# New step orders in the local transformers, and attention weights turned inside the normalisation

## Chip, cores and metric

The kernel runs on one core of one Trainium2 chip. The metric is the time of one execution on the device in microseconds (us), the median of several runs. TensorE (PE) multiplies, VectorE (DVE), ScalarE (ACT) and GpSimd (POOL) work on elements, and SyncE (SP) issues the transfers. The engines run at the same time, each through its own list of instructions in the order in which the program gives it, and wait for each other on semaphores.

## The reference

A network of eight sublayers on 8 sequences of 256 tokens with 128 channels, all in float32. Each is `x = x + f(layernorm(x))`:

```
x += mamba(ln(x));  x += local(ln(x));  x += dense_attention(ln(x));  x += local(ln(x))
x += linear_attention(ln(x));  x += fp4_ffn(ln(x));  x += head_attention(ln(x));  x += fp4_ffn(ln(x))

local(x): for each of 6 layers
    q, k, v = split(shift(x) @ Wqkv)                    # 16 heads of 64
    q, k = rotary(l2norm(q) * qs), rotary(l2norm(k) * ks)
    x = x + softmax(mask(q @ k.T * 8)) @ v @ Wo         # windows of 32, looking one window back
    xn = layernorm(shift(x)) * g + b
    x = x + (xn @ W1a + b1a) * gelu(xn @ W1g + b1g) @ W2 + b2
```

`dense_attention` attends over the 16 heads of each token, `linear_attention` is causal linear attention with softplus features, whose scale is `sqrt(8) * exp(beta)`; both project with three 128x128 matrices and end in a fourth.

## The kernel before

The stream `x` lies in `net.xT`, the normalised input in `net.zT`, channels on the partitions, all 8 sequences beside each other. The sublayers run one after the other, with a barrier of all engines between their blocks, and each begins with `normalise` (from L241). That centres the stream on TensorE (`centre`), squares it on ScalarE, takes the variance on TensorE, then eight warming matmuls (`warm`) that compute nothing that is used, while VectorE takes inverse roots (`inverse_root`). ScalarE has copied the centred stream to `net.zT` by then. The roots are transposed (L306), copied (L323), spread over the partitions on TensorE (L312) and multiplied in on VectorE (L337). `prefetch` issues the weights of the sublayer on SP meanwhile.

`local_transformer` (from L860) runs twice. One (layer, sequence) pair counts as one of SEQS = 48 sequences, since a sequence needs only its own result of the layer before. It is a pipeline written out by hand: each engine has a function `iteration` with its list of steps, and `run(step, lag, k)` does part k of the step for sequence n - lag in iteration n, if there is such a sequence. So a list with lags 2 to 6 has steps of five sequences between each other; in the first iterations (the fill) and the last (the drain) part of it is left out. There are 48 + TAIL = 54 iterations. Where a list is cut into iterations doesn't matter to its engine, only the resulting sequence of steps does. "`up 6,2`" below stands for `run(up, 6, 2)`.

The steps of one sequence, in the order of its data: `shift_in` (VectorE, L1501) makes the shifted input; `project` 0 to 7 (TensorE, L1208) makes q and k, `project_v` 0 to 3 (L1219) v; `square` (ScalarE, L1380), `sum_squares` (VectorE, L1524) and `root` 0 to 11 (GpSimd, L1122 and others) give the inverse norms; `rotate` (VectorE, two instructions, L1514 and L1517), `add_parts` (GpSimd, L1108) and `scale` (GpSimd, L1114) apply rotary and norms; `turn_qk` 0 to 3 (TensorE, L1269) transposes, `copy_qk` (ScalarE, L1414) copies back; `score` 0 to 3 (TensorE, L1233), `maxima` 0 to 7 (VectorE, L1533, four pairs of instructions), `exps` (ScalarE, L1397, four pairs), `recip` 0 to 3 (VectorE), `norm_p` 0 to 7 (GpSimd, L1135), `turn_probs` (TensorE, L1244), `copy_probs` (ScalarE), `weigh` 0 to 3 (TensorE, L1257), `copy_o` (VectorE, L1549), `out_project` in two parts (TensorE, L1279), `residual1` (VectorE). Then the feed-forward part, all in one PSUM bank `fb`: `centre` (TensorE, L1288), `square2` (ScalarE), `variance` (TensorE), `add_eps` (VectorE), `std` (GpSimd, L1130), `spread_std` (ScalarE), `spread` (TensorE), `affine` (VectorE), `bias_xn` (ScalarE), `up` 0 to 2 (TensorE, L1321), `gelu` 0 to 2 (ScalarE, L1442), `gate` 0 to 2 (VectorE, L1576), `down` (TensorE, L1330), `residual2` (VectorE, L1582; for the last eight sequences also L1586).

`project` and `project_v` take two PSUM banks in turn, in the order of the ring PROJECTIONS, and wait until the one before the last was rotated or copied; `turn_qk`, `score` and `turn_probs` take two pairs of banks in turn, in the order of PAIRS_OF_BANKS. `gelu` and `exps` need different tables on ScalarE, so each iteration loads a table twice. SP moves part of v (`move_v`) and loads the next layer's weights.

`dense_attention` (from L1647) and `linear_attention` load four weight matrices in `prefetch`, and transpose them on TensorE at the start of their own block (`turn_weights`, L1643), ahead of the first projection (L1700, L1905); ScalarE copies the result (L1734, L1955). In `linear_attention` ScalarE takes `exp(beta)` (L1953) ahead of that copy, with a table load.

## Time and profile before

| | |
|---|---|
| median of 3 runs | 4189.5 us (4188.85 to 4190.77) |
| profiled execution: time, span | 4191.06 us, 4189.2 us |
| TensorE (PE) busy | 92% of the span |
| VectorE, ScalarE, GpSimd busy | 84%, 80%, 81% |
| mean granted TensorE clock | 0.964 of full |
| first local transformer | 482.4 to 2073.5 us of the span |
| dense attention | 2073.5 to 2213.8 us |
| second local transformer | 2213.8 to 3804.1 us |
| linear attention | 3804.1 to 3909.1 us |

Busy time is the time in which an engine has at least one instruction under way. The ends of matmuls are modelled, so blocks on TensorE are best compared from start to start. A line of the timeline gives the start, the length, the engine, the line of the kernel, what is written from what, the shapes and the count of merged instructions; in brackets stands the idle time of the engine before it and what ended it.

### The profile page before, as it was taken

Reading aid. Unit: us, or ns where it says so; the run is one execution under the profiler, and the core shown is the slowest. Engines: PE = TensorE matmul, PEld = TensorE weight load, DVE = VectorE, ACT = ScalarE, POOL = GpSimd, SP = SyncE. Lnnn points to the kernel's source line nnn. Section 1 sums busy time; section 2 is a strip of 40 time slices with the busy share of each in tenths; the row PEclk is TensorE's granted clock in tenths of the full one; section 3 lists DMA queues with packets and bytes.
Section 4 is the critical chain, followed back from the end, with each engine's and each line's share of the span. In section 5 each row is a group of like instructions: output and inputs, shape, how many; then the busy total and the mean of one; then the engine's idle time right before and its main releaser. Section 6 shows DMA issues by size and latency. Waiting matters only on the chain. (4 is left out here: it accounts for less than half of the span.)

```text
span 4189.2 us, 141892 instructions
## 1 busy us (share of the span) xinstructions
PE 3839.1 (92%) x52653; PEld 2317.7 (55%) x52653; DVE 3525.8 (84%) x11433; ACT 3337.6 (80%) x10657; POOL 3391.1 (81%) x4093
## 2 busy tenths in 40 slices
PE   6888789999999999999767999999999999996686
PEld 2333356666666666666453666666666666663464
DVE  6999889899899899899476899899899899974646
ACT  6888589999999999999514999999999999983122
POOL 3999798998998998999296999999999999871324
PEclk8999999999999999999898999999999999997888
DMA  1000111111111111011002111111111111110000
GB/s 29 1 1 1 47 27 31 43 35 36 43 32 49 30 39 44 25 35 33 12 0 63 25 28 52 28 43 40 30 43 37 43 30 38 31 25 3 6 3 10
DMA packets 78611, 122.77 MB, mean 29 GB/s; under 512 B 26024, under 2 KB 47204, under 8 KB 77924
## 3 DMA queue, kind: packets, MB, share of 16 engines
q1 hardware_dynamic: 77924, 113.71, 10.4%
q8 instruction: 419, 6.86, 0.7%
...
## 5 line engine op out<-in xcount | busy, mean ns | idle before, releaser
L1397 ACT ACTIVATE local_pr<-local_tb,local_nmax 128x96 f32<-128x96 f32 x3072 | 1003.5, 368 | 179.1 <-DVE local_nmax L1533 172.2
L1108 POOL TENSOR_TENSOR local_qk<-local_qk,local_rb 128x512 f32<-128x512 f32 x768 | 975.0, 1281 | 107.9 <-DVE local_rb L1517 107.2
L1208 PE MATMUL local_pj<-local_wqkv,local_xs 128*64 128x512 f32 x3072 | 811.5, 607 | 27.1 <-DVE local_rb L1517 12.8
L1114 POOL TENSOR_TENSOR local_qk<-local_qk,local_rinv 128x512 f32<-128x512 f32 x768 | 791.7, 1047 | 7.5
L1397 ACT ACTIVATION_READ_ACCUMULATOR local_pr<-local_tb,local_nmax 128x1 f32 x3072 | 719.4, 234 | 0.0
L1533 DVE CUSTOM_DVE_ANT_0 local_tb<-local_tb,local_mask 128x96 f32<-128x96 f32 x3072 | 680.5, 291 | 5.7 <-PE local_tb L1233 5.7
L1524 DVE TENSOR_REDUCE local_ss<-local_sq 128x8 f32<-128x512 f32 x768 | 521.6, 680 | 183.3 <-ACT local_sq L1380 180.3
L1135 POOL TENSOR_TENSOR local_pr<-local_pr,local_rsum 128x384 f32<-128x384 f32 x768 | 624.3, 831 | 29.3 <-DVE local_rsum L1539 29.3
L1514 DVE TENSOR_TENSOR local_qk<-local_pj,local_rope 128x512 f32<-128x512 f32 x768 | 516.6, 673 | 56.0 <-ACT local_sq L1380 44.7
L1380 ACT ACTIVATE local_sq<-local_pj 128x512 f32<-128x512 f32 x768 | 499.2, 650 | 48.7 <-PE local_pj L1208 43.0
L1517 DVE TENSOR_TENSOR local_rb<-local_pj,local_rope 128x512 f32<-128x512 f32 x768 | 522.6, 680 | 0.0
L1257 PEld LDWEIGHTS local_ob<-local_prT,local_v 128*64 128x64 f32 x12288 | 427.3, 139 | 138.4 <-issue 109.4
L1405 ACT ACTIVATE local_prT<-local_tb 128x512 f32<-128x512 f32 x768 | 443.7, 672 | 1.9 <-PE local_tb L1244 1.9
L1533 DVE DVE_READ_ACCUMULATOR2_ANT local_nmax<- 128x1 f32 x3072 | 432.4, 141 | 0.0
L1257 PE MATMUL local_ob<-local_prT,local_v 128*64 128x64 f32 x12288 | 426.2, 223 | 0.0
L1219 PE MATMUL local_pj<-local_wqkv,local_xs 128*64 128x512 f32 x1536 | 404.4, 606 | 4.0 <-DVE local_rb L1517 4.0
L1279 PE MATMUL local_fb<-local_oT,local_wo 128*64 128x256 f32 x3072 | 372.3, 384 | 4.1 <-DVE net_zT L1582 4.1
L763 POOL TENSOR_TENSOR mamba_scan_drive<-mamba_u,mamba_scan_b_all 128x512 f32<-128x512 f32 x256 | 319.6, 1271 | 52.4 <-ACT mamba_scan_b_all L733 48.9
L1269 PEld LDWEIGHTS local_tb<-net_ident,local_qk 64*128 64x128 f32 x6144 | 223.2, 140 | 237.5 <-issue 82.8
L1233 PEld LDWEIGHTS local_tb<-local_kT,local_qT 64*64 64x64 f32 x12288 | 265.7, 133 | 122.9 <-ACT local_kT L1414 75.4
L1321 PE MATMUL local_fb<-local_xn,local_w 128*64 128x256 f32 x2304 | 310.1, 391 | 13.9 <-ACT local_g L1442 6.9
L1233 PE MATMUL local_tb<-local_kT,local_qT 64*64 64x96 f32 x12288 | 320.4, 247 | 0.8 <-ACT local_prT L1405 0.5
...
## 6 DMA issues: line engine op xcount, KB each, us to landing
...
```

The source lines that it names most:

```text
L1108: nc.gpsimd.tensor_tensor(qk[:, u, :], qk[:, u, :], rb[:, u % 2, :], ALU.add).then_inc(s["summed"], 1)
L1114: nc.gpsimd.tensor_tensor(heads8(qk[:, u, :]), heads8(qk[:, u, :]), r, ALU.mult).then_inc(s["scaled"], 1)
L1135: nc.gpsimd.tensor_tensor(at, at, view(rsum[:, k // 2, k % 2, 0:1], [[1, 4], [0, KW]]), ALU.mult).then_inc(s["weighted"], 1)
L1208: ins = nc.tensor.matmul(bank[own, :], xs[:, par, u // 4 * P + own.start:u // 4 * P + own.stop], wqkv[:, dep % 2, u % 4 * BANK:(u % 4 + 1) ...
L1233: ins = nc.tensor.matmul(sc[h][low * QB:(low + 1) * QB, i * KW:(i + 1) * KW], qT[own, par, p, q:q + QB], kT[own, par, p, q:q + KW], start= ...
L1257: ins = nc.tensor.matmul(ob[h * DH:(h + 1) * DH, i * P + low * QB:i * P + (low + 1) * QB], v[:, par, V_BLOCK[2 * t + low], 2 * (4 * half + ...
L1380: nc.scalar.activation(sq[:, u % 2, :], projection_bank("rotated", u)[:, :], ACT.Square).then_inc(s["squared"], 1)
L1397: ins = nc.scalar.activation(pr[:, (NU * c + k) % PR_RING, i, WIN:WIN + KW], scores[:, i * KW:(i + 1) * KW], ACT.Exp, scale=-1.0, bias=nma ...
L1514: nc.vector.tensor_tensor(heads8(qk[:, u, :]), heads8(bank[:, :]), cosines, ALU.mult)
L1517: nc.vector.tensor_tensor(rb[:, u % 2, :].rearrange("p (h a c) -> p h a c", a=2, c=DH // 2), swapped, sines, ALU.mult).then_inc(s["rotated ...
L1524: nc.vector.tensor_reduce(ss[:, par, 8 * u:8 * u + 8], heads8(sq[:, u % 2, :]), AX.X, ALU.add).then_inc(s["summed_sq"], 1)
L1533: ins = nc.vector.tensor_tensor_reduce(at, at, mask[:, k // 4, :], -1.0, 3.0e38, ALU.add, ALU.min, nmax[:, k, i:i + 1])
```

## The change

Four things, with no arithmetic added or removed. First, all engines' lists in the local transformer have a new order, and with them the rings of PSUM banks and the order on SP. Second, `dense_attention` and `linear_attention` hand their weights to `normalise`, which transposes them behind the variances, into bank 1 of `p_bc`, and then issues three warming matmuls instead of eight; ScalarE copies them ahead of its copies to `net.zT`. Third, in every `normalise` two of the four copies to `net.zT` now stand behind the copy of the roots, and VectorE waits for each. Fourth, linear attention's `exp(beta)` is taken in the normalisation, and `beta` is loaded first.

The lists of `iteration`, written short:

```
TensorE, before:
turn_probs 5,1; variance 6,0; project 3,2; turn_qk 4,2; score 4,0; project_v 4,2; spread 6,0; project_v 4,3; project 3,3; weigh 5,1; project 3,4;
turn_probs 5,2; turn_probs 5,3; project 3,5; up 6,0; weigh 5,2; project 3,6; turn_qk 4,3; turn_probs 4,0; up 6,1; project 3,7; score 4,1; score 4,2;
project_v 3,0; up 6,2; weigh 5,3; project_v 3,1; down 6,0; project 2,0; out_project 5,0; score 4,3; turn_qk 3,0; out_project 5,1; project 2,1; weigh
4,0; centre 5,0; turn_qk 3,1
TensorE, changed:
out_project 6,1; project 3,2; turn_qk 4,1; turn_probs 5,1; project_v 4,1; score 4,0; centre 6,0; project 3,3; weigh 5,0; project 3,4; variance 6,0;
turn_qk 4,2; weigh 5,1; project 3,5; turn_probs 5,2; turn_qk 4,3; spread 6,0; project 3,6; weigh 5,2; up 6,0; project 3,7; turn_probs 5,3; turn_probs
4,0; project_v 4,2; up 6,1; score 4,1; score 4,2; up 6,2; project_v 4,3; weigh 5,3; project_v 3,0; down 6,0; project 2,0; project 2,1; score 4,3;
turn_qk 3,0; out_project 5,0
ScalarE, before:
square 3,2; copy_qk 4,4; spread_std 6,0; copy_qk 4,5; copy_v 4,2; exps 4,0; copy_v 4,3; square 3,3; exps 4,1; square 3,4; bias_xn 6,0; copy_probs 5,4;
copy_probs 5,5; copy_probs 5,6; square 3,5; copy_probs 5,7; gelu 6,0; gelu 6,1; square 3,6; copy_qk 4,6; copy_qk 4,7; copy_probs 4,0; copy_probs 4,1;
gelu 6,2; square 3,7; exps 4,2; copy_v 3,0; exps 4,3; exps 4,4; exps 4,5; square 2,0; copy_v 3,1; copy_qk 3,0; copy_qk 3,1; exps 4,6; exps 4,7; square
2,1; square2 5,0; copy_qk 3,2; copy_qk 3,3; copy_probs 4,2; copy_probs 4,3
ScalarE, changed:
exps 5,3; copy_v 5,3; copy_v 4,0; exps 5,4; exps 5,5; square 3,0; square 3,1; copy_qk 4,0; exps 5,6; exps 5,7; copy_qk 4,1; square 3,2; copy_qk 4,2;
copy_qk 4,3; copy_probs 5,2; copy_probs 5,3; copy_v 4,1; square2 6,0; exps 4,0; square 3,3; exps 4,1; square 3,4; copy_qk 4,4; copy_qk 4,5; spread_std
6,0; square 3,5; copy_probs 5,4; copy_probs 5,5; copy_qk 4,6; bias_xn 6,0; copy_qk 4,7; square 3,6; gelu 6,0; square 3,7; gelu 6,1; copy_probs 5,6;
copy_probs 5,7; copy_probs 4,0; copy_probs 4,1; gelu 6,2; copy_v 4,2; exps 4,2
VectorE, before:
add_eps 6,0; sum_squares 3,1; copy_o 5,0; rotate 3,2; maxima 4,0; maxima 4,1; affine 6,0; shift_in 2,0; sum_squares 3,2; rotate 3,3; recip 4,0; copy_o
5,1; sum_squares 3,3; rotate 3,4; sum_squares 3,4; copy_o 5,2; sum_squares 3,5; rotate 3,5; rotate 3,6; sum_squares 3,6; gate 6,0; sum_squares 3,7;
rotate 3,7; maxima 4,2; gate 6,1; gate 6,2; maxima 4,3; maxima 4,4; residual2 6,0; maxima 4,5; copy_o 5,3; recip 4,1; sum_squares 2,0; maxima 4,6;
maxima 4,7; residual1 5,0; recip 4,2; rotate 2,0; recip 4,3; rotate 2,1
VectorE, changed:
recip 5,2; maxima 5,6; maxima 5,7; rotate 3,0; sum_squares 3,0; rotate 3,1; residual1 6,0; rotate 3,2; sum_squares 3,1; maxima 4,0; maxima 4,1;
sum_squares 3,2; recip 5,3; copy_o 5,0; rotate 3,3; add_eps 6,0; sum_squares 3,3; recip 4,0; rotate 3,4; copy_o 5,1; sum_squares 3,4; affine 6,0;
rotate 3,5; sum_squares 3,5; copy_o 5,2; rotate 3,6; sum_squares 3,6; sum_squares 3,7; rotate 3,7; gate 6,0; maxima 4,2; maxima 4,3; gate 6,1; gate
6,2; shift_in 2,0; maxima 4,4; maxima 4,5; residual2 6,0; copy_o 5,3; recip 4,1
GpSimd, before:
add_parts 4,6; root 4,0 to 4,11; scale 4,0; scale 4,1; scale 4,2; norm_p 5,2; norm_p 5,3; scale 4,3; add_parts 4,7; scale 4,4; scale 4,5; add_parts
3,0; std 6,0; norm_p 5,4; scale 4,6; norm_p 5,5; add_parts 3,1; norm_p 5,6; norm_p 5,7; add_parts 3,2; scale 4,7; norm_p 4,0; norm_p 4,1; add_parts
3,3; add_parts 3,4; add_parts 3,5
GpSimd, changed:
add_parts 4,6; root 4,0 to 4,11; scale 4,0; scale 4,1; norm_p 5,2; add_parts 4,7; scale 4,2; norm_p 5,3; scale 4,3; norm_p 5,4; add_parts 3,0;
add_parts 3,1; scale 4,4; add_parts 3,2; scale 4,5; norm_p 5,5; scale 4,6; scale 4,7; std 6,0; norm_p 5,6; add_parts 3,3; norm_p 5,7; norm_p 4,0;
add_parts 3,4; norm_p 4,1; add_parts 3,5
```

The rest of the diff, cut to its core:

```diff
-def normalise(net, tag, prefetch, beside_pool=None, beside_dve=None, late_pool=None):
+def normalise(net, tag, prefetch, beside_pool=None, beside_dve=None, late_pool=None, weights=None):
...
+        p_weights = p_bc[:, 1, :]
...
@@ -301,10 +302,14 @@
             for q in range(NC):
                 ins = variance(q)
             ins.then_inc(summed, 1)
-            warm(nc, net, p_idle, 8)
+            if weights:
+                weights.turn(pe, p_weights)
+            warm(nc, net, p_idle, 3 if weights else 8)
             pe.wait_ge(roots, 1 + ROOT_STEPS)
             nc.tensor.transpose(p_rootT, root[:, :], net.ident[:, :]).then_inc(turned, 1)
             pe.wait_ge(copied, 1)
+            if weights:
+                pe.wait_ge(weights.ready, 1)
             for pair in ((0, 1), (2, 3)):
                 for j in range(NT):
                     for q in pair:
@@ -317,10 +322,17 @@
             for q in range(NC):
                 act.wait_ge(centred, q + 1)
                 nc.scalar.activation(part(sq, q), p_cen[:, q, :], ACT.Square).then_inc(squared, 1)
-            for q in range(NC):
-                nc.scalar.activation(part(z, q), p_cen[:, q, :], ACT.Copy, scale=-1.0)
+            def keep(q):
+                nc.scalar.activation(part(z, q), p_cen[:, q, :], ACT.Copy, scale=-1.0).then_inc(kept, 1)
+
+            if weights:
+                weights.keep(act, p_weights)
+            for q in range(NC // 2):
+                keep(q)
             act.wait_ge(turned, 1)
             nc.scalar.activation(rootT[:, :], p_rootT, ACT.Copy).then_inc(copied, 1)
+            for q in range(NC // 2, NC):
+                keep(q)
 
         @block.vector
         def _(dve):
@@ -331,8 +343,8 @@
             dve.wait_ge(cleared, 1)
             dve.wait_ge(roots, 1)
             inverse_root(nc, dve, roots, 1, var[:, :, :], seed[:, :, :], by_tile(root[:, :]), [t[:, :, :] for t in tmp])
-            dve.wait_ge(copied, 1)
             for q in range(NC):
+                dve.wait_ge(kept, q + 1)
                 dve.wait_ge(spread, q // 2 + 1)
                 nc.vector.tensor_tensor(part(z, q), part(z, q), p_bc[:, q, :], ALU.mult)
     net.release_past()
...
-PAIRS_OF_BANKS = [("probs", 5, 1), ("qk", 4, 2), ("score", 4, 0), ("probs", 5, 2), ("probs", 5, 3), ("qk", 4, 3),
-         ("probs", 4, 0), ("score", 4, 1), ("score", 4, 2), ("score", 4, 3), ("qk", 3, 0), ("qk", 3, 1)]
-PROJECTIONS = [("rotated", 3, 2), ("v_ready", 4, 2), ("v_ready", 4, 3), ("rotated", 3, 3), ("rotated", 3, 4), ("rotated", 3, 5),
-         ("rotated", 3, 6), ("rotated", 3, 7), ("v_ready", 3, 0), ("v_ready", 3, 1), ("rotated", 2, 0), ("rotated", 2, 1)]
+PAIRS_OF_BANKS = [("qk", 4, 1), ("probs", 5, 1), ("score", 4, 0), ("qk", 4, 2), ("probs", 5, 2), ("qk", 4, 3),
+         ("probs", 5, 3), ("probs", 4, 0), ("score", 4, 1), ("score", 4, 2), ("score", 4, 3), ("qk", 3, 0)]
+PROJECTIONS = [("rotated", 3, 2), ("v_ready", 4, 1), ("rotated", 3, 3), ("rotated", 3, 4), ("rotated", 3, 5), ("rotated", 3, 6),
+         ("rotated", 3, 7), ("v_ready", 4, 2), ("v_ready", 4, 3), ("v_ready", 3, 0), ("rotated", 2, 0), ("rotated", 2, 1)]
...
                 run(move_v, 0, 0)
-                run(next_w1, 2, 0)
-                run(next_w2, 2, 0)
                 run(next_wo, 1, 0)
+                run(next_w1, 1, 0)
                 run(next_wqkv, -1, 0)
+                run(next_w2, 1, 0)
...
+class Weights:
+
+
+    def __init__(self, net, m, tag, first=None):
+        self.nc, self.ident, self.first = net.nc, net.ident, first
+        self.raw, self.kept = m.sb("w_in", [P, 4, C]), m.sb("wT", [P, 4, C])
+        self.loaded, self.turned, self.ready = (net.sem(f"{tag}_{n}") for n in ("w_in", "w_turned", "w_ready"))
+
+    def load(self, sp, sources):
+        for i, source in enumerate(sources):
+            sp.dma_start(self.raw[:, i, :], source).then_inc(self.loaded, 16)
+
+    def turn(self, pe, bank):
+        pe.wait_ge(self.loaded, 16 * 4)
+        for i in range(4):
+            ins = self.nc.tensor.transpose(bank[:, i * C:(i + 1) * C], self.raw[:, i, :], self.ident[:, :])
+        ins.then_inc(self.turned, 1)
+
+    def keep(self, act, bank):
+        if self.first:
+            self.first(act)
+        act.wait_ge(self.turned, 1)
+        self.nc.scalar.activation(self.kept[:, :, :].rearrange("p i c -> p (i c)"), bank, ACT.Copy).then_inc(self.ready, 1)
...
         @block.tensor
         def _(pe):
-            pe.wait_ge(w_in_ok, 16 * 4)
-            turn_weights(nc, pe, w_in, bank[7], net.ident, s["w_turned"])
-            pe.wait_ge(s["w_ready"], 1)
...
         @block.scalar
         def _(act):
-            act.wait_ge(s["w_turned"], 1)
-            nc.scalar.activation(wT[:, :, :].rearrange("p i c -> p (i c)"), bank[7][:, :], ACT.Copy).then_inc(s["w_ready"], 1)
...
+        grow = m.sb("grow", [P, 1])
+        cols_in, beta_in, grown = (net.sem(f"{tag}_{n}") for n in ("cols_in", "beta_in", "grown"))
+
+        def grow_scale(act):
+            act.wait_ge(beta_in, 16)
+            nc.scalar.activation(grow[:, :], cols[:, 4:5], ACT.Exp).then_inc(grown, 1)
+
+        weights = Weights(net, m, tag, grow_scale)
+        wT = weights.kept
 
         def prefetch(sp):
-            for i, name in enumerate("qkvo"):
-                sp.dma_start(w_in[:, i, :], d[f"{p_}W{name}"]).then_inc(w_in_ok, 16)
             with nc.allow_non_contiguous_dma(reason="one word per partition"):
+                beta = d[p_ + "beta"]
+                sp.dma_start(cols[:, 4:5], bass.AP(beta.tensor, beta.offset, [[1, NH], [0, HD], [1, 1]])).then_inc(beta_in, 16)
+                weights.load(sp, [d[f"{p_}W{name}"] for name in "qkvo"])
                 for i, name in enumerate("qkvo"):
                     sp.dma_start(cols[:, i:i + 1], d[f"{p_}b{name}"].rearrange("(p o) -> p o", o=1)).then_inc(cols_in, 16)
-                beta = d[p_ + "beta"]
-                sp.dma_start(cols[:, 4:5], bass.AP(beta.tensor, beta.offset, [[1, NH], [0, HD], [1, 1]])).then_inc(cols_in, 16)
-
-        normalise(net, tag, prefetch)
+
+        normalise(net, tag, prefetch, weights=weights)
```

In `linear_attention` the same lines go from the blocks of TensorE and ScalarE, VectorE takes `scale`, `shrink` and `shrunk_bias` ahead of its masks, and the first argument on ScalarE waits for the four biases.

## Rows read from the trace of the kernel before

**Rows 1.** The page, busy time, share of the span and instructions of each engine.

```profile
PE 3839.1 (92%) x52653; PEld 2317.7 (55%) x52653; DVE 3525.8 (84%) x11433; ACT 3337.6 (80%) x10657; POOL 3391.1 (81%) x4093
```

**Rows 2.** Timeline of VectorE: `residual2` of the first and forty-first sequence, first transformer.

```profile
610.58 0.48 DVE L1582 SCALAR_TENSOR_TENSOR net_zT<-local_fb,local_cols,local_z 128x256 f32<-128x256 f32 x1
...
1867.89 0.48 DVE L1582 SCALAR_TENSOR_TENSOR net_zT<-local_fb,local_cols,local_z 128x256 f32<-128x256 f32 x1
1868.40 1.03 DVE L1586 TENSOR_TENSOR net_xT<-net_xT,net_zT 128x256 f32<-128x256 f32 x1
```

**Rows 3.** Busy time in stretches: length, each engine, clock, DMA; middle and late period.

```profile
1128.40:1159.83 31.43, 31.43 (x518) 19.72 (x516) 28.32 (x108) 29.61 (x104) 28.62 (x38) 1.00 0.14 36
1867.90:1899.80 31.90, 31.39 (x518) 19.70 (x516) 29.30 (x109) 29.66 (x104) 28.80 (x38) 1.00 0.11 27
```

**Rows 4.** Timeline of TensorE in a middle period, two parts of it.

```profile
1134.40 1.03 PE L1208 MATMUL local_pj<-local_wqkv,local_xs 128*64 128x512 f32 x4
1135.37 0.71 PE L1269 MATMUL local_tb<-net_ident,local_qk 64*128 64x64 f32 x16
1135.91 0.66 PE L1244 MATMUL local_tb<-net_ident,local_pr 64*128 64x64 f32 x16
1136.50 1.08 PE L1321 MATMUL local_fb<-local_xn,local_w 128*64 128x256 f32 x8
1137.41 1.03 PE L1208 MATMUL local_pj<-local_wqkv,local_xs 128*64 128x512 f32 x4
1138.37 1.55 PE L1233 MATMUL local_tb<-local_kT,local_qT 64*64 64x96 f32 x64
1139.85 1.08 PE L1219 MATMUL local_pj<-local_wqkv,local_xs 128*64 128x512 f32 x4
...
1144.71 1.03 PE L1208 MATMUL local_pj<-local_wqkv,local_xs 128*64 128x512 f32 x4
1145.58 1.94 PE L1279 MATMUL local_fb<-local_oT,local_wo 128*64 128x256 f32 x16
1147.44 0.89 PE L1233 MATMUL local_tb<-local_kT,local_qT 64*64 64x96 f32 x32
1148.33 0.71 PE L1269 MATMUL local_tb<-net_ident,local_qk 64*128 64x64 f32 x16
```

**Rows 5.** Timeline of ScalarE and of VectorE in the same period: last `gelu`, first `gate`.

```profile
1138.71 0.50 ACT L1442 ACTIVATE local_g<-local_fb,local_cols 85x256 f32<-85x256 f32 x1
...
1139.25 0.48 DVE L1576 SCALAR_TENSOR_TENSOR local_g<-local_fb,local_cols,local_g 128x256 f32<-128x256 f32 x1 [0.36 <-ACT local_g L1442]
```

**Rows 6.** Busy time in stretches, as rows 3: second and third interval of the fill.

```profile
516.30:546.10 29.80, 19.83 (x226) 8.18 (x223) 20.46 (x72) 15.93 (x48) 26.88 (x41) 0.89 0.11 28
546.10:578.80 32.70, 26.51 (x434) 15.88 (x435) 25.07 (x100) 24.91 (x95) 30.39 (x45) 0.90 0.11 27
```

**Rows 7.** Busy time in stretches, as rows 3: last three intervals of the drain.

```profile
1994.20:2022.30 28.10, 23.94 (x478) 17.61 (x474) 14.64 (x82) 26.34 (x98) 17.84 (x23) 1.00 0.12 30
2022.30:2046.40 24.10, 18.11 (x293) 13.45 (x295) 11.45 (x57) 14.30 (x56) 5.44 (x7) 0.93 0.01 3
2046.40:2069.00 22.60, 13.36 (x89) 6.83 (x85) 4.78 (x11) 3.13 (x8) 0.69 (x1) 0.73 0.00 0
```

**Rows 8.** Timeline of TensorE and ScalarE, dense attention: turning, roots' copy, first projection.

```profile
2083.43 0.28 ACT L323 ACTIVATE dense_attn_ln_rootT<-dense_attn_ln_p_bc 128x128 f32<-128x128 f32 x1 [1.76 <-PE dense_attn_ln_p_bc L306]
...
2087.82 1.09 PE L1643 MATMUL dense_attn_bank<-net_ident,dense_attn_w_in 128*128 128x128 f32 x4 [2.34 <-PEq L56]
2089.60 1.01 PE L1700 MATMUL dense_attn_bank<-dense_attn_wT,net_zT 128*128 128x384 f32 x1 [0.69 <-ACT dense_attn_wT L1734]
```

**Rows 9.** Timeline of TensorE, linear attention, and busy time of a stretch, as rows 3.

```profile
3818.40 1.09 PE L1643 MATMUL linear_attn_bank<-net_ident,linear_attn_w_in 128*128 128x128 f32 x4 [2.34 <-PEq L56]
3820.40 1.22 PE L1905 MATMUL linear_attn_bank<-net_zT,linear_attn_wT 128*128 128x512 f32 x1 [0.91 <-ACT linear_attn_wT L1955]
...
3818.10:3824.90 6.80, 5.59 (x10) 2.64 (x11) 1.75 (x7) 3.42 (x5) 0.00 (x0) 0.50 0.00 0
```

227 lines of the change are left out of this document (106 added, 121 removed).

## Prediction

> **What bounds the kernel now.** I read the page first: TensorE is busy for 92% of the span, more than any other engine [rows 1]. An average over eight stages doesn't say where, so I cut the span into stretches. The two local transformers take 482.4 to 2073.5 us and 2213.8 to 3804.1 us, together three quarters of the span, and their inner part repeats exactly: the last step of a sequence, `residual2`, starts at 610.58 us for the first sequence and at 1867.89 us for the forty-first [rows 2], which is 1257.31 / 40 = 31.43 us for each. In one such period TensorE is busy 31.43 of 31.43 us at the full granted clock, ScalarE 29.61, VectorE 28.32 and GpSimd 28.62 [rows 3]. So TensorE bounds the middle, and the reader should see two things: no other engine is far behind, and there is no idle time on TensorE for a better order to remove. Only three things can then change with an order: what TensorE's own stream costs, the fill, and the drain.
>
> The timeline of TensorE shows that its stream does depend on the order [rows 4]. Its blocks use the array in three layouts: 128 rows (projections, `weigh`, `up`, `down`, `out_project`), 64x128 (both transposes) and 64x64 (`score`). Start to start, `project` followed by another full-height block takes 0.87 us (1144.71 to 1145.58). Followed by a transpose or a score it takes 0.96 to 0.97 (1134.40 to 1135.37, 1137.41 to 1138.37): **0.10 for going in**. A transpose followed by a transpose takes 0.54, followed by `up` 0.59, and that `up` takes 0.91 where eight matmuls of 256 columns are as many columns as four of 512, 0.86: **0.05 + 0.05 = 0.10 for coming out**, and I allow up to 0.15. Between the two small layouts a score followed by a transpose takes 0.89, and a score by itself 0.71 to 0.77, since two take 1.48 (1138.37 to 1139.85): about **0.12 to 0.18**.
>
> **Part 1, the orders in the steady state.** No instruction is added or removed, so the 37 blocks keep their own durations. I went round both lists and counted changes of layout. Before: six runs of small-layout blocks and two changes inside runs. Changed: seven runs (the lone `turn_qk 4,2` and the lone `score 4,0` are runs of their own) and one change inside. That is one run more, 0.20 to 0.25 us, less one inner change, 0.09 to 0.18: between +0.02 and +0.16 us a period. I take +0.09, the middle, so 31.52 us. Some 43 periods of each transformer run full, so +3.9 us each. Pairs of blocks that the trace of before doesn't have (`weigh` before `up`, `centre` before `project`, `out_project` before `out_project`) are all full-height to full-height, which rows price at nothing; I leave the same +0.02 to +0.16 for them.
>
> The Trainium skill speaks against this step. TensorEngine Tiling (Array Packing), section Key Properties, says that changing the tiling mode, not just the tile, drains TensorE. By that rule every change of layout pays, and the new list has 15 against 14. The rows agree that each costs 0.05 to 0.18; they don't show a full drain of the 1.03 us that one project block spans.
>
> Does another engine become late? I laid the three other lists beside TensorE's, with durations as in the trace. Their work stays 29.61, 28.32 and 28.62 of 31.52 us, so all fit if the order fits. The tightest place that I find is new: `up 6,2` follows `up 6,1` by only two scores, 0.96 + 0.71 + 0.77 = 2.44 us [rows 4], and it waits for `gate 6,0`, which waits for `gelu 6,2`, which waits for `up 6,1`: 1.08 for the matmuls, 0.50 gelu, 0.48 gate [rows 5] and three handovers of about 0.05, 2.2 us together. 0.24 us are left. Queued behind `up 6,2` on TensorE are `project_v 4,3` and all else, so nothing hides a miss here. Everything else has 0.4 us or more by my layout. On SP the weight loads for the next layer now wait one iteration earlier in its queue, so `move_v` stands behind them, once in eight sequences; the values that it moves are needed some 12 us later, and TensorE doesn't wait. I cost it at nothing.
>
> **Part 2, the last eight sequences.** There `residual2` has a second instruction, which takes 1.03 us where it is queued [rows 2], and the period is 31.90 us with TensorE no longer full [rows 3]: VectorE's chain sets the end, 0.5 us a period. In the new order VectorE idles after `recip 4,1`, which takes the instruction up, but GpSimd's `norm_p 5,2` waits for that same `recip` and hands the delay on to `turn_probs 4,0`. Between -2.0 us (all gone) and 0: I take -0.5 each.
>
> **Part 3, the fill.** In the second and third interval between first projections (516.3 to 546.1 and 546.1 to 578.8 us) GpSimd is the busiest engine, 26.88 of 29.80 and 30.39 of 32.70 [rows 6]. Its idle 2.9 + 2.3 = 5.2 us is the most that an order can take out here. In the new lists `project` of the next sequence's second block stands ahead of the transpose that it was behind, and `rotate 3,0` stands ahead of its `sum_squares`, so the sums for GpSimd come earlier and its idle time should mostly go. Between 0 and -5.2: I take -3.5 each.
>
> **Part 4, the drain.** The last three intervals from `down` to `down` take 28.1, 24.1 and 22.6 us [rows 7]. In the first ScalarE is busy 26.34 of 28.10, so at most 1.8 is to be had; the last is the bare serial chain of the feed-forward part, so the second can lose 24.1 - 22.6 = 1.5 at most, and the last nothing. Between 0 and -3.3: I take -2.0 each.
>
> **Part 5, the weights.** In dense attention the turning and its copy keep the first projection from 2087.82 to 2089.60 us [rows 8]: 1.78 us, which go. Moved into the normalisation, the four transposes take the place of five warming matmuls. ScalarE's copy stands ahead of the copy of the roots, but ScalarE had been idle 1.76 us there [rows 8], more than a copy needs; nothing is late. In linear attention it is 3818.40 to 3820.40, 2.0 us, and the table load for `exp(beta)` moves beside work too. But the granted clock is 0.50 until 3824.9 [rows 9], and an earlier start spends its gain on half-speed matmuls if the clock rises at the same moment: between -1.0 and -2.0, I take -1.5. Were the clock to fall inside the normalisations, with three warming matmuls instead of eight, about 1 us would be lost in each. Together -3.3. The other six normalisations only have two copies behind the roots' instead of ahead: nothing.
>
> **The sum.** Each transformer: +3.9 - 0.5 - 3.5 - 2.0 = -2.1, both -4.2; weights -3.3; together -7.5 us. The profiled execution took 4191.06 us (span 4189.2), so 4183.6 in its terms; it lies 1.6 above the median of the runs, 4189.5, so I predict **4182.0** (-0.18%). A measurement can tell about 0.2%, 8.4 us, from no change.
>
> **The rivals.**
> - *A, the stream is no dearer and fill and drain give all.* 31.43 us a period, -0.5, -5.2 and -3.3: -9.0 each, -18.0, and -3.3: 4168. For it: the new lists keep producers and consumers closer. Against it: the extra run of small-layout blocks.
> - *B, only TensorE's stream changes.* Fill and drain are chains of waits that any order has: +3.9 - 0.5 = +3.4 each, -3.3: 4193. That is also the time if the change doesn't do what it is described to do. For it: the last drain interval is bare chain.
> - *C, layout changes cost more.* The extra run costs its whole 0.25 and nothing comes back: +10.8 - 0.5 - 5.5 = +4.8 each, -3.3: 4196. This is the rule of Key Properties above, worked out from rows.
> - *D, slower: `up 6,2` waits for `gate 6,0`.* Every 0.1 us by which the chain exceeds its 2.44 us costs 86 x 0.1 = 8.6 us, as TensorE has no idle time to take it up. At 0.3 us over: -7.5 + 25.8, 4208. It decides from 0.19 us over (15.9 / 86), a chain of 2.63 us instead of 2.2.
>
> **How the numbers follow.** Forecast 0.33 (own range 4175 to 4189), A 0.22, B 0.18, C 0.13, D 0.14. Faster by over 0.2% is under 4181.1: A, and a bit over half of the forecast, 0.40. Slower is over 4197.9: D and an edge of C, 0.16. Within: 0.44. The range reaches past A, 4164 for a price of layout below my least, and past C to 4198; D and what is beyond A stay out, 0.2.
>
> **What the changed profile would show.** Right: one period between 31.45 and 31.60 us with TensorE busy throughout; `turn_qk 4,2` between two blocks that start 0.1 us late; the interval of the fill with GpSimd nearly full; dense attention's first projection 1.7 us sooner after its normalisation begins. Wrong: TensorE idle ahead of `up`, released by VectorE's `gate` (D); a period of 31.6 or more with TensorE full (C); fill and drain as long as before (B); a period under 31.4, which would mean that I mispriced pairs of blocks. A stall at any place that my layout left 0.4 us would make the prediction wrong most cheaply, since 86 periods repeat it.

## The result, and the profile after

The changed kernel takes **4196.45 us** (median of 16 runs, 4192.94 to 4201.19), the kernel before 4189.98 beside it: a ratio of 1.0017 (95% interval 1.0010 to 1.0024). The forecast was 4182.0 and faster; the kernel is slower by 6.5 us, which lies within my range and on the wrong side of no change. The profiled execution is the slowest of the sixteen, 4201.19 us with a span of 4199.4, 4.7 above the median, so sums from its trace come out that much too large. Two executions of all that are compared below stand far off, one of 9539.78 us in experiment 2 and one of 4662.23 with the weights alone in experiment 5; the ratios leave them out.

The page's busy row of the changed kernel, to be read against [rows 1]:

```profile
PE 3853.0 (92%) x52643; PEld 2345.5 (56%) x52643; DVE 3545.5 (84%) x11433; ACT 3349.2 (80%) x10657; POOL 3388.6 (81%) x4093
```

The shares say nothing: 92, 84, 80 and 81% against 92, 84, 80 and 81. The stretches do. First `residual2` of the first and the forty-first sequence on VectorE's timeline, as in [rows 2]:

```profile
609.26 0.48 DVE L1594 SCALAR_TENSOR_TENSOR net_zT<-local_fb,local_cols,local_z 128x256 f32<-128x256 f32 x1
...
1877.53 0.48 DVE L1594 SCALAR_TENSOR_TENSOR net_zT<-local_fb,local_cols,local_z 128x256 f32<-128x256 f32 x1
```

(1877.53 - 609.26) / 40 = **31.71 us** a period, against 31.43 before. The first sequence ends 1.3 us sooner than before, the forty-first 9.6 us later. Busy time in stretches (length, then PE, PEld, DVE, ACT, POOL, clock, DMA), one middle period, the two intervals of the fill and the three of the drain, as [rows 3], [rows 6] and [rows 7]:

```profile
1129.36:1161.07 31.71, 31.62 (x523) 20.03 (x521) 28.65 (x108) 29.74 (x104) 28.60 (x38) 1.00 0.14 36
...
515.20:546.40 31.20, 20.84 (x224) 9.14 (x225) 20.65 (x74) 16.95 (x54) 28.40 (x45) 0.84 0.01 1
546.40:577.00 30.60, 25.27 (x432) 14.80 (x433) 24.43 (x100) 24.82 (x93) 29.12 (x42) 0.94 0.11 29
...
2002.80:2030.40 27.60, 24.82 (x481) 17.45 (x479) 13.05 (x75) 24.88 (x89) 15.55 (x18) 1.00 0.12 31
2030.40:2053.40 23.00, 18.18 (x303) 13.23 (x300) 10.37 (x47) 14.31 (x56) 5.44 (x7) 0.93 0.15 37
2053.40:2075.90 22.50, 13.23 (x91) 6.63 (x87) 4.78 (x11) 3.14 (x8) 0.69 (x1) 0.73 0.00 0
```

In the period TensorE is again full, or nearly: 31.62 of 31.71 us. A matmul that waits inside a group is counted as busy, so this row can't tell a dear stream from a stalled one. The drain has 73.1 us for 74.8.

**Where the 0.28 us of a period come from.** I laid TensorE's blocks start to start. All but two pairs have the price that rows 4 let expect. The two that don't are `score 4,1` to `score 4,2`, 0.92 us, and `score 4,2` to `up 6,2`, 0.95, where rows 4 have 0.71 and 0.77. TensorE's timeline, changed kernel:

```profile
1136.51 1.04 PE L1333 MATMUL local_fb<-local_xn,local_w 128*64 128x256 f32 x8
...
1140.37 1.03 PE L1333 MATMUL local_fb<-local_xn,local_w 128*64 128x256 f32 x8
1141.34 1.81 PE L1245 MATMUL local_tb<-local_kT,local_qT 64*64 64x96 f32 x64
1143.21 1.08 PE L1333 MATMUL local_fb<-local_xn,local_w 128*64 128x256 f32 x8
```

These are `up 6,0`, `up 6,1`, two scores and `up 6,2`. The two scores take 1.81 us where [rows 4] have 1.55 for the same 64 matmuls: the second stood in the middle of the row. Now ScalarE's timeline of the same moment, and VectorE's `gate 6,0`:

```profile
1136.31 0.60 ACT L1392 ACTIVATE local_sq<-local_pj 128x512 f32<-128x512 f32 x1
1137.63 1.28 ACT L1454 ACT_TABLE_LOAD   x1 [0.72 <-PE local_fb L1333]
1138.93 0.47 ACT L1454 ACTIVATE local_g<-local_fb,local_cols 128x256 f32<-128x256 f32 x1
1139.30 0.59 ACT L1392 ACTIVATE local_sq<-local_pj 128x512 f32<-128x512 f32 x1
1139.78 0.48 ACT L1454 ACTIVATE local_g<-local_fb,local_cols 128x256 f32<-128x256 f32 x1
1140.13 2.07 ACT L1417 ACTIVATE local_prT<-local_tb 128x512 f32<-128x512 f32 x4
1142.05 0.50 ACT L1454 ACTIVATE local_g<-local_fb,local_cols 85x256 f32<-85x256 f32 x1
```

```profile
1142.58 0.48 DVE L1588 SCALAR_TENSOR_TENSOR local_g<-local_fb,local_cols,local_g 128x256 f32<-128x256 f32 x1 [0.77 <-ACT local_g L1454]
```

Read it from the end. `up 6,2` starts at 1143.21, 0.15 behind the gate's end at 1143.06. The gate waited for `gelu 6,2`. `score 4,2` needs the pair of banks that the last of the four `copy_probs` frees; that ends at 1142.20 and the score starts at 1142.26. Both hang on ScalarE, which works without a pause from 1137.63 on, and what it starts with is **the load of gelu's table, 1.28 us, which waited 0.72 us for `up 6,0`**: `up 6,0` ends at 1137.55. A table load reads nothing that `up` writes. It needn't have waited.

The kernel text shows why it did. `gelu` with j = 0 has two waits in a row, first for `down_ready`, then for `up_ready` (`need` is a wait that is left out where there is nothing to wait for yet). In the trace's record of the queue, the first wait in program order is carried by the activation itself; the second is an instruction of its own, it ends at 1137.59, and the compiler's table load stands behind it. This is the theory that the experiments test; call it the held load. The groups of the profile (line, engine, operation, count, busy us, mean ns, idle before and who ended it) name it in one line. The loads for gelu, changed kernel and then kernel before:

```profile
L1454 ACT ACT_TABLE_LOAD x94 | 120.6, 1283 | 67.4 <-PE local_fb L1333 67.4
```

```profile
L1442 ACT ACT_TABLE_LOAD x94 | 120.6, 1283 | 1.7
```

67.4 us over 94 loads is 0.72 each, and it was nothing before: there ScalarE came to the gelu long after `up 6,0` was done, so the same two waits in the same order cost nothing.

**The weights.** TensorE's timeline of dense attention, changed kernel: the four transposes of the weights, the transposed roots, their spreading, the first projection (to be read against [rows 8]):

```profile
2087.78 0.66 PE L1667 MATMUL dense_attn_ln_p_bc<-net_ident,dense_attn_w_in 128*128 128x128 f32 x4
...
2089.87 0.33 PE L309 MATMUL dense_attn_ln_p_bc<-net_ident,dense_attn_ln_root 128*128 128x128 f32 x1 [0.79 <-DVE dense_attn_ln_root L206]
2090.56 2.85 PE L317 MATMUL dense_attn_ln_p_bc<-dense_attn_ln_rootT,net_pick 32*128 32x128 f32 x32 [0.37 <-ACT dense_attn_ln_rootT L333]
2095.28 0.98 PE L1725 MATMUL dense_attn_bank<-dense_attn_wT,net_zT 128*128 128x384 f32 x1 [1.87 <-PEq L56]
```

From the stage's first matmul (2080.40) to the first projection it is 14.88 us, before 16.05 (2073.55 to 2089.60). The 1.78 us of turning are gone, but the spreading takes 2.85 us where it took 1.72: the granted clock is 0.54 in 2090.5 to 2095.3. In linear attention the spreading takes 1.72 and the first projection comes 14.33 us after the stage's first matmul for 16.26. The first projection isn't the end of it, as the clock stays at half beyond it (0.50 until 2100.4). From its first matmul to that of the next sublayer, dense attention takes 139.8 us for 140.2 and linear attention 102.4 for 105.0.

### The profile page after: what moved, and what is told of

Its sections match the earlier page's. It is cut to its first block and busy times, and to the rows that moved or that the text cites. A ratio compares the mean times of both kernels' runs of the same rounds, so it can differ in the third digit from the quotient of the medians.

```text
span 4199.4 us, 141906 instructions
## 1 busy us (share of the span) xinstructions
PE 3853.0 (92%) x52643; PEld 2345.5 (56%) x52643; DVE 3545.5 (84%) x11433; ACT 3349.2 (80%) x10657; POOL 3388.6 (81%) x4093
## 5 line engine op out<-in xcount | busy, mean ns | idle before, releaser
L1220 PE MATMUL local_pj<-local_wqkv,local_xs 128*64 128x512 f32 x3072 | 787.4, 601 | 34.8 <-DVE local_rb L1529 17.6
L1147 POOL TENSOR_TENSOR local_pr<-local_pr,local_rsum 128x384 f32<-128x384 f32 x768 | 636.3, 836 | 208.9 <-DVE local_rsum L1551 208.9
L1409 ACT ACTIVATION_READ_ACCUMULATOR local_pr<-local_tb,local_nmax 128x1 f32 x3072 | 750.5, 244 | 0.0
L1392 ACT ACTIVATE local_sq<-local_pj 128x512 f32<-128x512 f32 x768 | 475.6, 647 | 117.1 <-PE local_pj L1220 117.1
L1417 ACT ACTIVATE local_prT<-local_tb 128x512 f32<-128x512 f32 x768 | 416.0, 632 | 0.3
L1231 PE MATMUL local_pj<-local_wqkv,local_xs 128*64 128x512 f32 x1536 | 411.8, 608 | 2.6 <-DVE local_rb L1529 2.6
L1291 PE MATMUL local_fb<-local_oT,local_wo 128*64 128x256 f32 x3072 | 352.7, 382 | 1.3 <-DVE net_zT L1594 1.3
L1245 PE MATMUL local_tb<-local_kT,local_qT 64*64 64x96 f32 x12288 | 341.0, 249 | 2.5
L1333 PE MATMUL local_fb<-local_xn,local_w 128*64 128x256 f32 x2304 | 310.3, 390 | 18.1 <-ACT local_g L1454 5.6
L1220 PEld LDWEIGHTS local_pj<-local_wqkv,local_xs 128*64 128x64 f32 x3072 | 213.8, 138 | 171.3 <-issue 63.8
```

Of the source, the lines that this page charges most:

```text
L1147: nc.gpsimd.tensor_tensor(at, at, view(rsum[:, k // 2, k % 2, 0:1], [[1, 4], [0, KW]]), ALU.mult).then_inc(s["weighted"], 1)
L1220: ins = nc.tensor.matmul(bank[own, :], xs[:, par, u // 4 * P + own.start:u // 4 * P + own.stop], wqkv[:, dep % 2, u % 4 * BANK:(u % 4 + 1) ...
L1245: ins = nc.tensor.matmul(sc[h][low * QB:(low + 1) * QB, i * KW:(i + 1) * KW], qT[own, par, p, q:q + QB], kT[own, par, p, q:q + KW], start= ...
L1392: nc.scalar.activation(sq[:, u % 2, :], projection_bank("rotated", u)[:, :], ACT.Square).then_inc(s["squared"], 1)
L1409: ins = nc.scalar.activation(pr[:, (NU * c + k) % PR_RING, i, WIN:WIN + KW], scores[:, i * KW:(i + 1) * KW], ACT.Exp, scale=-1.0, bias=nma ...
```

## The experiments

**1. The two waits exchanged, in the changed kernel.**

```
             def gelu(e, par, j):
+                act.wait_ge(s["up_ready"], 3 * e + (1 if j < 2 else 2))
                 if j == 0:
                     need(act, s["down_ready"], e)
-                act.wait_ge(s["up_ready"], 3 * e + (1 if j < 2 else 2))
```

> The kernel after, with the two waits ahead of the first gelu exchanged: first for the up-projection, then for the previous down-projection (which is long done). Theory T (the table): in the kernel after the load of gelu's table stands behind the wait for up 6,0, because that wait is the second of two; it starts 0.7 us late, and the chain table 1.28 us, two gelus, a square, four copy_probs pushes score 4,2 by 0.21 us and, by gelu 6,2 and the gate, up 6,2 by 0.17 us, in each of some 86 periods. With the waits exchanged the load is issued while up 6,0 still runs: the period falls from 31.71 to 31.33-31.45 us and the time from 4196 to about 4166 (4162 to 4176), below both kernels. Rival R (the stream of the new orders is dearer by its changes of array layout, or both stalls come from the ring of bank pairs and the gate themselves): which wait stands first changes nothing, the period stays at 31.7 and the time at 4194 to 4198. Rival S (the table is the cause but the next chain takes its place): the period falls by under 0.15 us, time 4184 to 4192.

Measured: **4158.25 us**, ratio 0.9929 to the kernel before (0.9916 to 0.9941), 38 us below the changed kernel and 31 below the kernel before. ScalarE's timeline, TensorE's, the period's stretch and the group of the gelu loads:

```profile
1099.60 0.60 ACT L1392 ACTIVATE local_sq<-local_pj 128x512 f32<-128x512 f32 x1
1100.22 1.28 ACT L1454 ACT_TABLE_LOAD   x1
```

```profile
1099.80 1.04 PE L1333 MATMUL local_fb<-local_xn,local_w 128*64 128x256 f32 x8
...
1104.64 1.55 PE L1245 MATMUL local_tb<-local_kT,local_qT 64*64 64x96 f32 x64
1106.12 1.08 PE L1333 MATMUL local_fb<-local_xn,local_w 128*64 128x256 f32 x8
```

```profile
1108.82:1140.13 31.31, 31.31 (x523) 19.55 (x520) 28.56 (x108) 29.90 (x103) 28.61 (x38) 1.00 0.14 36
```

```profile
L1454 ACT ACT_TABLE_LOAD x94 | 120.6, 1283 | 2.8 <-PE local_fb L1333 1.2
```

The load now starts with the end of the square, while `up 6,0` runs (1099.80 to 1100.84). The scores are back to 1.55 us, `score 4,2` to `up 6,2` to 0.77, and the period is 31.31. 0.21 + 0.18 us of stalls are gone, which is 31.71 - 31.31 = 0.40. The gain is a little more than my 4162 to 4176: the period is below the 31.33 that I had as its least, and the drain gained too (below). The held load is the cause; rivals R and S are out.

**2. The same exchange in the kernel before.**

> The kernel before with the same exchange of waits. Theory T: there the gelu comes late enough after up 6,0 that its table load waits for nothing (it starts 1.9 us or more behind the end of up 6,0), so nothing changes: 4190, within 0.1%. Rival U (a wait carried by the activation itself is cheaper on ScalarE in general): the time falls by some 8 us (0.1 us a period) or more here too.

4191.44 us, ratio 1.0000 (0.9991 to 1.0009). Nothing changes, so it isn't that one form of wait is cheaper than the other. Of the two orders, the exchange helps only the one that puts the gelu close behind its up-projection.

**3. Another cure.** The waits stay as they are in the changed kernel; one small gelu that waits for nothing stands ahead of them.

```
                 if j == 0:
+                    nc.scalar.activation(touch[:, :], net.ident[:, 0:1], ACT.Gelu)
+                if j == 0:
                     need(act, s["down_ready"], e)
```

> The kernel after, waits as they are, with one more activation ahead of the first gelu's waits: gelu of one column of the identity into a column of its own. It waits for nothing, so the table is loaded for it while up 6,0 runs. Theory T (what costs is when the table load starts, not the form of the wait): the load starts within 0.1 us of the end of square 3,6, as with exchanged waits; the period is 31.31 us plus at most the extra instruction's 0.2 us of ScalarE where that is on the path: time 4158 to 4170. Rival W (a semaphore wait carried by the activation is what makes it quicker): 4194 to 4200, since the waits stand as in the kernel after.

4156.84 us, ratio 0.9924 (0.9912 to 0.9936). ScalarE's timeline:

```profile
1097.30 0.60 ACT L1393 ACTIVATE local_sq<-local_pj 128x512 f32<-128x512 f32 x1
1097.92 1.28 ACT L1453 ACT_TABLE_LOAD   x1
1099.21 0.20 ACT L1453 ACTIVATE local_touch<-net_ident 128x1 f32<-128x1 f32 x1
1099.32 0.46 ACT L1457 ACTIVATE local_g<-local_fb,local_cols 128x256 f32<-128x256 f32 x1
```

Two cures that share nothing but an early load give the same time. The extra instruction costs 0.1 us of ScalarE from start to start, and ScalarE has it to spare.

**4. The same fault made at the other load.** In the kernel before, the wait for the maxima moves from first to last ahead of `exps`.

```
-                act.wait_ge(s["maxed"], NU * c + k + 1)
                 need(act, s["probs_turned"], (NU * c + k - PR_RING) // 2 + 1)
                 need(act, s["sum_inv"], COUPLES * (c - 1) + k // 2 + 1)
+                act.wait_ge(s["maxed"], NU * c + k + 1)
```

> The kernel before with the waits ahead of exps reordered: the wait for the maxima, first before, comes last. This makes the same fault at the other table load of the period. Theory T: the load for exps 4,2, which starts at 1139.71 us in the trace of before and lies under the wait that ends at 1142.52, is held until that wait ends; exps 4,2 starts 1.28 us later. ScalarE has 1.8 us idle in a period and 1.5 of it is at this place, so it loses most of its room; TensorE should wait for some of it: period 31.5 to 32.1 us, time 4196 to 4245, my value 4215. Rival W (held loads cost nothing here, or the load isn't held): 4190.

**4322.69 us**, ratio 1.0323 (1.0309 to 1.0337): 133 us slower, where I had put 25 down as most likely and 55 as the most. The group of these loads, and then one of them and the block of TensorE that pays:

```profile
L1397 ACT ACT_TABLE_LOAD x92 | 118.0, 1283 | 263.0 <-DVE local_nmax L1533 263.0
```

```profile
1135.86 1.28 ACT L1397 ACT_TABLE_LOAD   x1 [2.89 <-DVE local_nmax L1533]
```

```profile
1139.18 0.65 PE L1208 MATMUL local_pj<-local_wqkv,local_xs 128*64 128x512 f32 x2 [1.02 <-ACT local_v L1388]
```

The load is held 2.89 us, `exps 4,2` comes 1.28 us late, `copy_v` behind it on ScalarE too, and TensorE's next projection waits 1.02 us for the bank that this copy frees. The period grows to 32.95 us, by 1.52. I had reckoned that ScalarE's 1.8 us of idle time would take part of it up. They took nothing: 1.5 of them lay under the very wait that now stands ahead of the load, and the work behind it had no room of its own. The mechanism is the same as in the changed kernel, four times as dear.

**5. The orders alone, and the weights alone.**

> The kernel before with the changed orders of the local transformer alone; weights and normalisations as before. By the traces the two transformers are 7 us longer each, so theory T and every theory that puts the loss into the orders gives 4189.98 + 14 = 4204, less what the first stages of the profiled run had by chance (4199 to 4205). Rival V (the loss lies in the normalisations and the orders gain): below 4190.

> The kernel before with the weights of dense and linear attention turned within their normalisations, orders as before. My sum said -3.3 us (dense -1.8, linear -1.5). The traces say -0.5 for dense, where TensorE's clock falls to half in the middle of the normalisation and the spreading of the roots takes 2.85 us for 1.72, and -2.6 for linear: 4187.0. Rival V: 4195 or more.

Orders alone: 4204.19 us, ratio 1.0037 (1.0025 to 1.0050), with 31.71 us a period. Weights alone: 4185.92, ratio 0.9991 (0.9982 to 1.0000). So the orders cost 14.9 us and the weights give 3.4. Their sum, 4200.8, is 4 us above the changed kernel's 4196.45; the executions of one kernel lie 2 to 8 us apart, and I can't say more about those 4 us. The weights' 3.4 us aren't made as the two stages of the changed kernel are. In the trace of the weights alone the clock fell in linear attention's normalisation and not in the dense one: dense attention takes 135.7 us for 140.2, linear attention 105.9 for 105.0. The period of the old orders is 31.47 us there, and in experiment 2 as well, for 31.43 in the kernel before; that is 3 us over 86 periods, and no run tells why.

**6. The price of a change of layout.** My prediction counted changes and priced each at 0.10. One pair is exchanged here: `turn_qk 4,2` ahead of `variance` instead of behind it.

```
-                run(variance, 6, 0)
                 run(turn_qk, 4, 2)
+                run(variance, 6, 0)
```

> The kernel after with exchanged waits, and in TensorE's order turn_qk 4,2 ahead of variance 6,0 instead of behind it. The change counts are the same. My prediction priced every entry into a small layout at 0.10 us. The trace with exchanged waits has 0.025 for the entry behind variance and 0.96 - 0.86 = 0.10 for the one behind project. Theory P (the entry's price hangs on the block ahead of it): project to turn_qk 0.96, turn_qk to variance 0.59, variance to weigh 0.254, 1.80 in place of 0.861 + 0.279 + 0.641 = 1.78: period up by 0.02 to 0.03 us, some 2 us. Rival Q (one price for each entry): no change in the period beyond 0.01 us. Time 4158 to 4162 either way, if turn_qk 4,2's input is there 0.25 us sooner; if not, TensorE waits for ScalarE or GpSimd and the trace shows it.

4162.00 us, ratio 0.9937 (0.9924 to 0.9951); 31.37 us a period. TensorE's timeline with exchanged waits alone (first), and with this pair exchanged (second): `project`, `variance`, `turn_qk`, `weigh` against `project`, `turn_qk`, `variance`, `weigh`.

```profile
1123.97 1.03 PE L1220 MATMUL local_pj<-local_wqkv,local_xs 128*64 128x512 f32 x4
1124.83 0.35 PE L1307 MATMUL local_fb<-net_mean,local_sq 128*64 128x1 f32 x8
1125.11 0.71 PE L1281 MATMUL local_tb<-net_ident,local_qk 64*128 64x64 f32 x16
1125.75 1.15 PE L1269 MATMUL local_ob<-local_prT,local_v 128*64 128x64 f32 x32
```

```profile
1122.09 1.03 PE L1220 MATMUL local_pj<-local_wqkv,local_xs 128*64 128x512 f32 x4
1123.05 0.71 PE L1281 MATMUL local_tb<-net_ident,local_qk 64*128 64x64 f32 x16
1123.69 0.40 PE L1307 MATMUL local_fb<-net_mean,local_sq 128*64 128x1 f32 x8
1123.94 1.13 PE L1269 MATMUL local_ob<-local_prT,local_v 128*64 128x64 f32 x32
```

From `project` to `weigh` it is 1.78 us in the first and 1.85 in the second. (The same lists gave 31.31 to 31.32 us in each transformer of experiments 1, 3 and 8 with the load on time, so 0.06 is more than they scatter.) Going from `project` into the small layout costs 0.10 (0.96 for 0.86), going in from `variance` 0.03 (0.28 for 0.25). The counts of layout changes are the same, and the period differs by 0.06 us. An entry has no single price; reading P was right in kind and put the size at 0.02 to 0.03 us, as it took 0.59 for the way from `turn_qk` to `variance`, which is 0.64.

**7. One run of small-layout blocks less.** `turn_qk 4,2` goes behind `project 3,5`, next to `turn_probs 5,2` and `turn_qk 4,3`; first with ScalarE's two copies of it moved behind `square 3,5`, then with ScalarE's order left alone and, beside it, the eight warming matmuls of experiment 8.

```
                 run(variance, 6, 0)
-                run(turn_qk, 4, 2)
                 run(weigh, 5, 1)
                 run(project, 3, 5)
+                run(turn_qk, 4, 2)
                 run(turn_probs, 5, 2)
```

> The kernel after with exchanged waits, and the lone turn_qk 4,2 behind variance moved behind project 3,5, where turn_probs 5,2 and turn_qk 4,3 follow: one run of small-layout blocks less. ScalarE's two copies of it move behind square 3,5. Theory P (prices per pair of blocks, from the trace with exchanged waits): variance 0.279 + turn_qk 0.641 + project 0.962 + turn_probs 0.547 = 2.43 us become 0.254 + 0.96 + 0.55 + 0.55 = 2.31, so the period falls by 0.12 us to 31.19 and the time by 10 us to 4148. Rule Q of my prediction, where a run costs 0.20 to 0.25 us: period 31.06 to 31.11, time 4138 to 4141. If another engine has become the bound (ScalarE is the fullest) the period stays at 31.31 and TensorE waits: 4158.

> Exchanged waits, eight warming matmuls, and turn_qk 4,2 moved behind project 3,5 on TensorE alone; ScalarE keeps its order, so copy_qk 4,4 and 4,5 still stand ahead of spread_std. With ScalarE's copies moved too, turn_qk 4,3 stood 1.19 us for its pair of banks: the ring has two pairs, turn_qk 4,3 takes that of turn_qk 4,2, and the copies that free it ended at 1119.81 us behind spread_std and square 3,5. Reading G (the ring of two pairs is what the place has to fit): the two copies take 1.1 us from the end of turn_qk 4,2, and between it and turn_qk 4,3 lies only turn_probs 5,2, 0.55 us, so that TensorE still waits about 0.5 us; less the 0.12 us that one run of small-layout blocks saves, the period is 31.31 + 0.4 = 31.7 us (31.5 to 31.9), time 4172 to 4207, my value 4190. Reading H (the loss came from ScalarE's moved copies alone, and the gain of the run is to be had): 31.19 us, 4147.

4285.10 us (ratio 1.0229, 1.0215 to 1.0242) and 4260.83 (1.0173, 1.0159 to 1.0187). Both miss what I expected. In the first, with 32.62 us a period, `turn_qk 4,3` waits for the copies of `turn_qk 4,2`: it starts 1.74 us behind `turn_probs 5,2` for 0.55. The second, TensorE and then ScalarE:

```profile
1115.92 0.71 PE L1281 MATMUL local_tb<-net_ident,local_qk 64*128 64x64 f32 x16
1116.47 0.66 PE L1256 MATMUL local_tb<-net_ident,local_pr 64*128 64x64 f32 x16
1117.82 0.71 PE L1281 MATMUL local_tb<-net_ident,local_qk 64*128 64x64 f32 x16 [0.68 <-ACT local_qT L1426]
```

```profile
1116.68 1.09 ACT L1426 ACTIVATE local_qT<-local_tb 128x512 f32<-128x512 f32 x2 [1.36 <-PE local_tb L1281]
```

The ring has two pairs of banks. `turn_qk 4,2` starts at 1115.92 and ends at 1116.63, its two copies run from 1116.68 to 1117.77, and `turn_qk 4,3`, which needs the pair, starts at 1117.82: 0.80 us later than the 0.55 behind `turn_probs` at which it could. Reading G named this wait and sized it at 0.5, because I counted the copies from the end of the transposes but the room from their start. The rest of the +1.08 us a period is smaller waits. One is 0.24 us for `project 3,5`, which now comes nearly a microsecond earlier: `weigh 5,1` to `project 3,5` takes 1.17 us for 0.93. VectorE's second `rotate` ends at the time at which the projection starts, so I take the ring of projection banks for it; no run tested that alone. The gain of the run less, 0.12 us, could not be had here, and its size was not measured.

**8. Warming matmuls.** `warm(nc, net, p_idle, 8)` instead of 3 behind the turned weights, in the changed kernel and with exchanged waits.

> The kernel after with eight warming matmuls instead of three behind the turned weights. In the traces the clock fell inside the dense normalisation of after (the 32 spreading matmuls took 2.85 us for 1.72), and inside the linear one when the weights were changed alone, but in neither with the exchanged waits. Theory X (the idle 0.8 us ahead of the transposed roots decides whether the clock falls): 32 spreading matmuls take 1.72 us in both normalisations, and the time is 1 us below after's 4196.5. Rival Y (the fall is a matter of when the stage starts): it strikes one of them all the same. The time can't tell 1 us, the trace can.

> The kernel after with exchanged waits and eight warming matmuls in the two normalisations. So far the clock fell while the roots were spread in four of ten normalisations with three warming matmuls behind the turned weights, and in none of the two with eight. Theory X (eight keep it up): 1.72 us for the 32 spreading matmuls in both, first projection 14.4 us after the stage's first matmul. Rival Y (it is a matter of when the stage starts): one of them at 2.85 to 3.1. The time is 4157 to 4159 either way, as exchanged waits alone had no fall in either.

4198.07 us (ratio 1.0020, 1.0011 to 1.0029) and **4156.60** (0.9920, 0.9906 to 0.9933). The times tell nothing from 4196.45 and 4158.25. The traces tell a little: with three warming matmuls the clock fell in five of the twelve normalisations of weights (spreading 2.85 to 3.10 us: dense in the changed kernel, in 3 and in 6, linear with the weights alone and in the first of 7); with eight in none of six (1.72 each). The idle 0.79 us ahead of the transposed roots is filled then, and TensorE works on until they are turned. This fits reading X, but six cases are few, and the idle stretch alone doesn't decide it, as the other seven with three warming matmuls had it too. For the stages as a whole it is less clear. Dense attention takes 137.3 to 139.8 us in the three traces with one and 134.2 to 136.4 in the six without, linear attention 102.9 and 105.9 in the two with one and 102.3 to 102.8 in the seven without. So a fall may cost from a few tenths to some 3 us in a stage, and the medians don't show it.

## Why the prediction was wrong, point by point

- **What bounds the kernel: right.** TensorE without idle time for 86 periods; every tenth of a microsecond on it counts 8.6 us. The traces of the two kernels are 10.2 us apart: the period makes 24 more (86 times 0.28), and the last eight sequences, the fill, the drain and the two attentions give some 14 back.
- **"Everything else has 0.4 us or more by my layout": this step failed.** For the period the prediction names one wait that could come late, that of `up 6,2`, and prices every other at nothing. It says nothing of the table loads, so it took gelu's for work that never waits. In the trace of before that is how it looks: the gelu load group has 1.7 us of idle time in 94 loads. But there it had nothing to wait for by then. In the new order ScalarE is through with the square ahead of `gelu 6,0` at 1136.91, and `up 6,0` at 1137.55, so the wait that stands ahead of the load became real: 0.72 us late, of which 0.40 reach TensorE, 86 times 0.40 = 34 us. The medians of the changed kernel and experiment 1 are 38 us apart, their traces 43: these 34, and 3.8 more in each drain (73.1 us for 69.3).
- **`up 6,2` behind `gate 6,0`: the right place, for another reason.** I had 2.2 us for the chain in a gap of 2.44. The gate is indeed what `up 6,2` waits for, by 0.18 us (rival D put 0.3 over), because ScalarE is late as a whole. With the load on time the gate ends soon enough for the 0.77 us that a score takes by itself.
- **The stream's price: wrong sign.** I counted one run of small-layout blocks more and took +0.09 us a period, 31.52. Experiment 1 shows the stream by itself: 31.31, which is -0.12. Over 86 periods that is 18 us to the good, and without the held load the time is below my best case A, 4168, and below my range. The count was right, the price per entry wasn't: in the order of before, `score` behind `out_project` cost 0.09 to 0.14 (1.87 us for 1.78 or 1.73) and `turn_qk` behind `centre` 0.11, while the new `turn_qk 4,2` behind `variance` costs 0.03. Experiment 6 shows the spread between two such entries at 0.06 us a period. Start to start and by kind of block, experiment 1 against the kernel before, `out_project` takes 0.14 us a period less, `centre` and `turn_probs` 0.11 each and the scores 0.06; `up` takes 0.10 more, `spread` 0.05, `turn_qk` and `weigh` 0.04 each. So the gain is spread over the list, and no single entry makes it. The drain rule of the Trainium skill (TensorEngine Tiling (Array Packing), Key Properties), which would make each change of mode pay, agrees in kind, as every entry costs something; as a count of changes it gives the wrong sign here, and the measurement decides.
- **The last eight sequences: sized too small.** The four intervals behind the forty-first sequence take 126.8 us for 127.8, which is four plain periods of 31.71: the excess of 0.5 us a period is gone altogether, the end of my range where all goes. With the load on time they take 125.5, 0.07 a period above the plain ones.
- **The fill: sized too large.** -3.5 forecast, -1.3 measured. In the two intervals that I looked at GpSimd's idle time went from 5.2 us to 4.3 only and the two got 0.7 us shorter; the interval ahead of them, which my sum left out, gave 1.1 (19.3 us for 20.4), and the next interval, which I had not looked at, got longer by 0.4. Its stretch, changed kernel and then kernel before:

```profile
577.00:609.00 32.00, 31.68 (x516) 20.05 (x518) 27.93 (x107) 30.13 (x104) 30.53 (x39) 1.00 0.11 27
```

```profile
578.80:610.40 31.60, 31.45 (x518) 19.87 (x520) 27.36 (x102) 29.77 (x105) 28.77 (x39) 1.00 0.11 27
```

  GpSimd has 1.8 us more to do in it, 30.5 for 28.8. The lists move its work about between sequences, and I had counted the idle time that could go and not the work that comes.
- **The drain: right by chance.** -2.0 forecast, -1.7 measured (74.8 to 73.1). With the load on time it is -5.5, more than my bound of 3.3. The second interval, stretches with exchanged waits, against [rows 7]:

```profile
2013.40:2033.60 20.20, 16.71 (x300) 11.96 (x294) 10.27 (x46) 14.17 (x56) 5.44 (x7) 1.00 0.17 42
```

  20.2 us, where I held the 22.6 of the last interval for the bare chain that nothing can undercut. It isn't a floor: the granted clock is 0.73 in that last interval and 1.00 in this one. The same clock is part of the gain. In both transformers of the kernel before, the changed kernel and the orders alone it falls to half near the end of the second interval (0.86 to 0.93 in the mean, 22.9 us in the changed kernel), and in the six kernels with the load on time it doesn't fall there (1.00, 20.2 to 20.3 us); TensorE's busy time in it goes from 18.1 to 16.7. So of the 2.7 us some 1.4 are the clock by this estimate, and that the earlier load is what kept the clock up was not tested by itself.
- **The weights: the sum right, its parts not.** -3.3 forecast, -3.4 measured alone. Up to the first projection dense attention gives 1.2 us with the fallen clock and 1.7 without it (experiment 8), linear attention 1.9. But the whole stages, where I had -1.8 and -1.5, changed by -0.4 and -2.6 in the changed kernel, and by -4.5 and +0.9 with the weights alone. The granted clock in dense attention's first 4 us is 0.53 in the kernel before, 0.54 in the changed kernel and 1.00 with the weights alone; how much of such differences is the clock's doing was not tested, and that -3.4 meets -3.3 is in part luck. The fall inside a normalisation, which I named at about 1 us, came in one of the two each time.
- **The chances.** Slower by over 0.2% had 0.16; the result, +0.17%, lies just inside "within", where I had 0.44. The forecast's own range (4175 to 4189) missed. The time is near rival C's 4196, and C is wrong as a reason: layout changes did not cost more, they cost less. Its sign, a period of 31.6 us or more with TensorE full, came all the same, since a stall inside a group of matmuls counts as busy; so that sign couldn't tell a dear stream from a stall. Two errors with opposite signs stand behind a miss of 14 us: 24 us of gain that I didn't see (4182 to 4158), and 38 us of a stall that I had excluded.

**The best version.** Exchanged waits, with or without the eight warming matmuls, 4156.6 to 4158.3 us, and the small gelu instead, 4156.8: all three 0.7 to 0.8% faster than the kernel before, and no run tells them apart.
